# Two attention layers of a gated block: output projections as three reduced-precision products, Q two groups ahead in a ring

## What is computed

```python
x = x + tanh(g_xattn[0]) * attn0(layernorm(x), ctx)   # 16 heads of 32, biases
x = x + tanh(g_ffn[0])   * ffn0(layernorm(x))         # routed, 256 tokens a sequence
x = x + tanh(g_xattn[1]) * attn1(layernorm(x), ctx)   # 16 heads of 64
x = x + tanh(g_ffn[1])   * ffn1(layernorm(x))         # ternary weights, conv

def attn(x, ctx):                  # attn0 and attn1 alike
    q = x @ Wq;  k, v = ctx @ Wk, ctx @ Wv
    p = softmax(q @ k.T * dh ** -0.5)      # per head, over 128 context tokens
    return (p @ v) @ Wo + bo
```

## Time and profile before

| | us |
|---|---|
| median of 3 executions | 2031.3 |
| lowest, highest | 2029.82, 2041.83 |
| the profiled execution | 2034.14 |
| its span, first to last instruction | 2032.4 |
| PE busy in it | 1643.6 (81%) |
| DVE busy | 1249.5 (61%) |
| ACT busy | 817.9 (40%) |
| POOL busy | 542.0 (27%) |

### The profile page before, as it was taken

One profiled execution on the slowest core, in us unless ns is written; L12 is line 12 of the kernel. 1 busy time (PEld: TensorE's weight loads), 2 busy tenths in 40 slices (PEclk: granted clock), 3 DMA queues, 4 the chain that ended last, 5 costly groups with the idle time before them and its releaser, 6 DMA issues. The chain is left out here.

```text
span 2032.4 us, 23886 instructions
## 1 busy us (share of the span) xinstructions
PE 1643.6 (81%) x8804; PEld 876.0 (43%) x8804; DVE 1249.5 (61%) x1984; ACT 817.9 (40%) x1253; POOL 542.0 (27%) x472
## 2 busy tenths in 40 slices
PE   5788889884426788966999999999998557888887
PEld 3444444431203563425555555545443233444443
DVE  3577887785681343413546556556555449999996
ACT  3444444430561452304333233233222047777774
POOL 3122222220011210012121111111101048777771
PEclk9899998998667999987999999999999879999999
DMA  4012222112800243522011020110100140111121
GB/s 161 18 42 84 83 83 83 63 63 83 321 17 25 73 131 100 161 88 106 4 43 52 21 73 16 59 54 20 52 32 21 62 167 21 58 58 58 63 77 43
DMA packets 77666, 144.23 MB, mean 71 GB/s; under 512 B 12529, under 2 KB 21925, under 8 KB 77050
## 3 DMA queue, kind: packets, MB, share of 16 engines
q1 hardware_dynamic: 76602, 139.68, 20.0%
q0 software_dynamic: 960, 3.15, 0.5%
HBM read 99.78 MB, written 43.03 MB: 70 GB/s over the span
## 5 line engine op out<-in xcount | busy, mean ns | idle before, releaser
L561 PE MATMUL D_TX<-D_wo,D_oT 128*128 128x512 f32 x384 | 170.3, 597 | 2.5 <-DVE D_res L701 1.6
L515 ACT ACTIVATE D_probs<-D_SC 128x512 f32<-128x512 f32 x128 | 66.1, 603 | 223.1 <-PE D_SC L623 223.1
L1676 POOL TENSOR_TENSOR E_y<-E_y,E_centre 128x1024 f32<-128x1024 f32 x64 | 151.6, 2368 | 12.1 <-ACT E_y L1703 10.1
L1601 PE MATMUL E_OP<-E_w2q,E_yb 128*128 128x512 bf16 x512 | 130.5, 414 | 26.0 <-ACT E_yb L1688 21.8
L1592 PE MATMUL E_HP<-E_xT,E_w1q 128*128 128x512 bf16 x512 | 124.3, 387 | 9.0 <-DMA E_w1q<-w1b_d 6.1
L785 DVE TENSOR_TENSOR D_oT<-D_OB,D_rz 128x512 f32<-128x512 f32 x64 | 44.0, 688 | 133.3 <-PE D_OB L590 132.9
L1668 POOL TENSOR_SCALAR E_centre<-E_hs,E_cw,E_cb 128x512 f32<-128x512 f32 x64 | 107.8, 1684 | 63.9 <-DVE E_hs L1748 63.6
L552 PE MATMUL D_PJ<-D_xT_high,D_wq_high 128*128 128x512 f32 x236 | 101.9, 432 | 20.2 <-POOL D_xT_low L414 7.9
L419 POOL TENSOR_TENSOR D_rstd<-D_var,minus_half 128x1 f32<-128x1 f32 x32 | 17.4, 545 | 377.1 <-DVE D_var L707 377.1
L561 PEld LDWEIGHTS D_TX<-D_wo,D_oT 128*128 128x128 f32 x384 | 71.4, 191 | 85.3 <-issue 82.0
L1757 DVE SCALAR_TENSOR_TENSOR E_y<-E_hs,E_cw,E_y 128x512 f32<-128x512 f32 x128 | 107.2, 877 | 0.0
(11 more groups left out here) (332 smaller groups left out, 3739.8 us busy)
## 6 DMA issues: line engine op xcount, KB each, us to landing
A_x<-in_x SPq DMA_DIRECT2D x8, 1024.0 KB, 5.3
A_res<-in_x SPq DMA_DIRECT2D x8, 1024.0 KB, 5.8
x_d<-A_res SPq DMA_DIRECT2D x8, 1024.0 KB, 4.3
xn_d<-A_xn SPq DMA_DIRECT2D x8, 1024.0 KB, 8.3
W_raw<-in_w1T SPq DMA_DIRECT2D x16, 512.0 KB, 4.2
W_raw<-in_w2T SPq DMA_DIRECT2D x16, 512.0 KB, 4.2
D_x<-x_d SPq DMA_DIRECT2D x8, 1024.0 KB, 5.6
D_res<-x_d SPq DMA_DIRECT2D x8, 1024.0 KB, 5.7
```

What stands on the lines that cost most here:

```text
L515: act.activation(pr[:, g, :], SC[:, g, :], ACT.Exp, scale=scale).then_inc(s_ex, 1)
L561: mm = pe.matmul(out_banks[c], oT[par][:, k, c * P:(c + 1) * P], wo[:, k, :], start=k == 0, stop=k == QT - 1)
L1601: mm = pe.matmul(OP[:, :], yb[:, k, c * P:(c + 1) * P], w2q[:, k, :], start=k == 0, stop=k == MC - 1)
L1676: pool.tensor_tensor(y, y, U[i % 2][:, :, :], ALU.add).then_inc(t0, 1)
```

## The change

- **Output in three products.** Wo, scaled, is split into high (ACT) and low (POOL), the attention output too, and `project_out` makes three f32r matmuls where there was one in f32. The split of Wo is done in groups 0 and 1 of step 0.
- **Where the halves are made.** First layer: DVE divides into a buffer "o" of one tile, ACT makes the high half (`high_o`), POOL the low half (`low_o`). Second layer: DVE divides in place in bank OB, ACT makes the high half from it, DVE the low half; the next `weigh` may overwrite OB only then.
- **Second layer by halves of the heads.** A chunk of the output is now two units of four Q tiles' width each, added to the residual one after the other. Two units stand in each group, in banks ZB and PJ: at j == 2 and 3 the first half of this step, at j == 0 and 1 the second half of the step before. After step 7 four units are left.
- **Q two groups ahead.** Q is kept in a ring of 2 x QG tiles; group j makes Q of group j + 2. x of step n + 1 is transposed at j == 1 of step n, its statistics are taken at j == 3 and applied at j == 0, and x is loaded for step n + 2 after these transposes.
- **The lists.** ACT has high_o between guess_rz and keep_mT (in the second layer also one at the end of the group). POOL's list now goes by group. Ahead of step 0 only RING tiles of Q are made, and only the x of step 0 is transposed.

```diff
+        RING, OT = 2 * QG, QT // QG
+        woh, wol = sb("wo_high", [P, QT, D], F32R), sb("wo_low", [P, QT, D], F32R)
...
-        qh, ql = sb("q_high", [P, QT, TILE], F32R), sb("q_low", [P, QT, TILE], F32R)
-        oT = [sb(f"oT{i}", [P, QT, TILE]) for i in range(2)]
+        qh, ql = sb("q_high", [P, RING, TILE], F32R), sb("q_low", [P, RING, TILE], F32R)
+        oT = sb("oT", [P, 2, 2, OT, TILE], F32R)
+        of = sb("o", [P, TILE]) if QG == 1 else None
...
+        def q_ahead(lap, par, j):
+            return (2 * lap + par, lap, par, j + 2) if j < 2 else (2 * lap + par + 1, lap + par, par ^ 1, j - 2)
+        def out_units(lap, par, j):
+            if QG == 1:
+                return [(-1, 0, j, PJ[:, :] if j == 1 else TXF)]
+            back, half = (-1, 1) if j < 2 else (0, 0)
+            return [(back, half, 2 * (j % 2) + i, (ZB, PJ)[i][:, :]) for i in range(2)]
...
@@ sync, step @@
-                if not is_last(lap, par, 3):
-                    wait_apart(sp, x_tr, SUB * (n + 3), sp_passed)
-                    load_x(lap + 1 + par, par ^ 1)
+                if not is_last(lap, par, 2):
+                    wait_apart(sp, x_tr, SUB * (n + 2), sp_passed)
+                    load_x(lap + 1, par)
...
@@ gpsimd, step @@
+                for j in range(GROUPS):
+                    turn_x = j == 1 and not last
+                    if turn_x:
+                        low_x(n + 1, 0)
+                    if turn_x and QG == 1:
+                        low_x(n + 1, 1)
+                    if QG == 1:
+                        low_o(n, par, j)
+                    if turn_x and QG > 1:
+                        low_x(n + 1, 1)
+                    if first and j < 2:
+                        low_wo(j)
+                    if j == 0:
+                        add_bias(lap, par, (0, 1))
+                    if j == QG:
+                        add_bias(lap, par, (2, 3))
+                    if turn_x:
+                        low_x(n + 1, 2)
+                        low_x(n + 1, 3)
+                    if j == GROUPS - 1 and not is_last(lap, par, 2):
                         ln_rstd(n + 2)
                     if not first:
+                        for back, half, c, bank in out_units(lap, par, j):
+                            if half == QG - 1:
+                                post_rstd(n + back, c)
...
@@ scalar, step @@
+                    if more_q:
+                        keep_q(qn, QG * qj)
+                    if turn_x and QG == 1:
+                        keep_xT(n + 1, 0)
                     guess_rz(n, j)
+                    if isinstance(lap, int) and n == 0 and j < 2:
+                        split_wo(j)
+                    if QG > 1 and more_q:
+                        keep_q(qn, QG * qj + 1)
                     if turn_x:
+                        keep_xT(n + 1, 2 - QG)
+                    if turn_x and QG > 1:
+                        high_o(n, par, j, 0)
+                        keep_xT(n + 1, 1)
+                    if turn_x and QG == 1:
+                        high_o(n, par, j, 0)
+                        keep_xT(n + 1, 2)
+                    if not turn_x:
+                        high_o(n, par, j, 0)
                     if j < GROUPS - 1 or not last:
                         keep_mT(GROUPS * n + j + 1)
+                    if turn_x and QG > 1:
+                        keep_xT(n + 1, 2)
                     if turn_x:
+                        keep_xT(n + 1, 3)
+                    if QG > 1:
+                        high_o(n, par, j, 1)
...
@@ tensor @@
+            def project_out(i, k0, c, bank, part, parts):
+                for k in range(part * OT // parts, (part + 1) * OT // parts):
+                    for o, w in ((oh, woh), (oh, wol), (ol, woh)):
+                        mm = pe.matmul(bank, o[i][:, k, c * P:(c + 1) * P], w[:, k0 + k, :],
+                                       start=k == 0 and o is oh and w is woh, stop=k == OT - 1 and o is ol)
...
+                    if QG > 1:
+                        need(pe, fin, UNITS * n + 2 * j - SUB)
+                    if more_q:
+                        project_q(qn, QG * qj)
...
@@ vector, step @@
                     divide(n, par, j, 0)
+                    if j == 0 and not last:
+                        ln_apply(n + 1)
+                    if QG > 1:
+                        low_o(n, j, 0)
+                    if ahead and j == GROUPS - 1:
+                        ln_stats(n + 2, lap + 1, par)
+                    if QG > 1 and not first and j in (1, 2):
+                        for c in (2 * j - 2, 2 * j - 1):
+                            finish(*back1, c)
+                    for back, half, c, bank in [] if first and (QG == 1 or j < 2) else out_units(lap, par, j):
+                        add_out(n + back, par if back == 0 else par ^ 1, half, c, bank)
+                        if half == QG - 1:
+                            measure(n + back, par ^ 1, c)
+                    if QG == 1 and not first and j:
+                        finish(*back1, j - 1)
                     if QG > 1:
                         divide(n, par, j, 1)
+                        dve.wait_ge(o_ok, QT * n + QG * (j + 1))
+                        low_o(n, j, 1)
+                if not first and QG == 1:
+                    finish(*back1, SUB - 1)
```

More of the change, by code:

```diff
@@ L420, in post_rstd, with add_bias @@
                     .then_inc(p_rs, 1)
+            def add_bias(lap, par, chunks):
+                pool.wait_ge(r_in[par], 16 * (lap + 1))
+                for c in chunks:
+                    pool.tensor_tensor(R[par][:, c, :], R[par][:, c, :], bo[:, :], ALU.add).then_inc(biased, 1)
             ln_rstd(0)
@@ L432, in _, with low_wo @@
             pool.wait_ge(bo_ok, 1)
+            def low_wo(part):
+                for k in range(part * QT // 2, (part + 1) * QT // 2):
+                    pool.wait_ge(wo_hi, k + 1)
+                    pool.tensor_tensor(wol[:, k, :], wo[:, k, :], woh[:, k, :].bitcast(F32), ALU.subtract).then_inc(wo_lo, 1)
             def step(lap, par):
                 n = 2 * lap + par
-                first = isinstance(lap, int) and n == 0
-                for c in range(SUB):
-                    if c == 1 and not is_last(lap, par, 2):
+                first, last = isinstance(lap, int) and n == 0, is_last(lap, par, 1)
+                for j in range(GROUPS):
[18 more added lines that the diff above has]
+                    if j == GROUPS - 1 and not is_last(lap, par, 2):
@@ L670, in step @@
+                    if turn_x and not units:
+                        transpose_x(n + 1, 2)
+                        transpose_x(n + 1, 3)
+                    elif turn_x and QG == 1:
+                        transpose_x(n + 1, 3)
                     if QG > 1:
@@ L795, in _ @@
             maxima(0)
+            ln_stats(1, 0, 1)
             def step(lap, par):
```

246 lines of the change are left out of this document (132 added, 114 removed).

## The result

The changed kernel takes 2084.8 us in the median of four executions (2080.99 to 2087.73), beside 2032.9 for the kernel before: 1.0235 times as long, with a 95% interval of 1.0206 to 1.0263. The ratios of this document are those of means; the medians alone give 1.0255. The forecast was 2061, slower, range 2010 to 2095. The direction and the two mechanisms came true, the size of the loss in the first layer was too small.

The account below looks back on a forecast made before the run. PE bounds the second layer; in the first, PE and DVE are both near their limit. Second layer -24 and first +55 give +31, rounded to 30: 2064 us profiled, 2061 by the median, 1.5% slower; range 2010 to 2095.

Parts of the forecast that it names:

- the two mechanisms: First layer: POOL's wait for the residual closes a loop, and keep_mT waits on ACT behind high_o; layer sum +55 us.
- The loop of the first layer: Store, residual load, POOL's bias adds, low halves of x, Q, next store: binds steps 2 to 6 at 62.9 us each.
- the x loads: Sign of being right: in the first layer they come 62 to 64 us apart from step 2 on.
- Steps 0, 1 and 7 of the first layer: Step 0 goes from 45.2 to 59.1 us (+14), step 1 takes 53.1, step 7 and the end +3.
- The maxima behind the high half: First layer, ACT: keep_mT waits for divide and high_o, so a group takes 11.8 us instead of 10.56.
- The second layer: Sum -24 us: steps 1 to 6 -29, ahead of step 0 -17, step 0 +24, step 7 and the end -2.
- The products: Second layer: three f32r matmuls at 0.70 us replace one f32 at 0.886, -6.0 us a step.
- The wait for x: Second layer, j == 0: PE's wait for the last quarter of x goes away, -2.5 us a step.
- The new waits: Second layer: PE waits for late exps, 2.4 us after j == 1 and 1.3 after j == 2, +3.7 a step.
- The rival in which every group pays 1.4 us: First layer: idle PE lowers the clock in every group, 28 groups add 39 us, 2100 us in all; chance 0.15.
- Blocking of DVE by POOL: First layer: new low_o on POOL may hold DVE's last finish 1 us, 5 us more in all; left out of sum.
- The sentence on four passes: Output products: three of true FP32's four passes would make 0.66 us, 3 us more gain than 0.70; not used.

Follow-up runs that it names:

- the kernel with both edits of the first layer: Changed kernel; in the first layer POOL's bias adds end its step list and ACT copies transposed maxima ahead of o's high half: 2032.7 us, ratio 0.9975.

## Why the prediction was right, and where it was short

- *The loop of the first layer.* Right, term by term: store issued at +7.7 (forecast 7.7), residual in hand at +27.8 (27.1), last low half of x at +40.5 (39.0), low half of Q at +46.4 (44.2), next S at +53.1 (51.1), end of the step at +64.7 (62.9). Moving the bias adds takes it away and 46 us with it. Of the signs that it named, only the x loads missed, with 64 to 65 us between them instead of 62 to 64.
- *Its size.* The term that was too small is the sum after the residual is in hand: 11.9 us for POOL's list and 5.2 for the Q tile. POOL's items came to 12.6, because beside DVE's finish (1.38, 1.64, 1.76 us for its three parts) the low half of o took 1.73 us and the second pair of bias adds 2.93, instead of 1.27 and 2.5. The Q tile took 5.8 us, at the clock of 0.50 that the two holes had left. With 0.7 us more for the DMA that is 2.1 us, of which the last group gave 0.2 and the way from there to S 0.2 back; over steps 2 to 6 the excess is (65.2 - 62.9) x 5 = 12 us.
- *Steps 0, 1 and 7 of the first layer.* Step 0 was 64.6, forecast 59.1, its groups 14.0, 15.4, 20.7 and 14.5 against 13.8, 13.85, 19.65 and 11.8. Half of the excess is in the last group: PE without output products is often idle, has 2.8 us of idle time released by A_mT ahead of the next S and starts it at the slow clock (0.80 us for a first row that takes 0.51 at full clock). Step 1 was 56.5 (53.1); 2.3 us of that are its first group, whose S and first Q products ran at this clock. These 9 us are most of the rest of the miss. Their mechanism, the queue on ACT, is confirmed by the run that reorders ACT: step 0 falls by 9.6 us and step 1 by 2.6.
- *The maxima behind the high half.* Right: an ordinary group is 11.65 us from S to S (forecast 11.8, 10.56), with 1.34 us of idle PE released by A_mT. But within the loop the order costs only 0.9 us a step, as the same run shows.
- *The second layer.* -23 against a forecast of -24, by errors that cancel. The products gave 5.2 us of PE a step, not 6.0: a half chunk takes 2.89 us, so a chunk 5.78 against 7.09, and three f32r matmuls 0.72 with their starts, not 0.70. The run with one f32 product has PE busy 5.0 us longer and its step 4.0. The wait for x went (2.5). The new waits were 1.1 us a step and not 3.7: the finishes took 2.5 to 2.9 us, not 3.05, and at j == 2 nothing was late. A step won 5.8 us instead of 4.8. Step 0 cost 28 instead of 24, 9.0 us of it the wait for divide and low half behind the split of Wo, where I had 6.
- *The clock.* The rival in which every group pays 1.4 us did not happen: from 290 to 301 the clock is 1.00. It is low behind the two long holes of a step, and for a few us behind the 2.75 us at j == 0 (0.51 from 247.5 to 251), where the loop hides it.
- *Blocking of DVE by POOL.* I left it out of the sum. In the changed kernel that was nearly right, since DVE idles for 10.7 us behind it. It became the largest cost, 17 to 31 us, only once the loop was gone. The Trainium skill (SBUF — State Buffer, Who interferes with whom) gives as reason a pair of SBUF ports that DVE and GpSimd share, and excepts a DVE instruction with one SBUF input outside the two-port modes; the traces agree with both halves, 0.69 to 1.63 us for the product with two SBUF inputs, and no change for the statistics and for the low half of Q, which has one input in PSUM (0.75 us beside a POOL instruction too). The norm has one SBUF input and went from 0.54 to 1.48; that fits only if it ran in a two-port mode, which no trace here shows. The same section says that the second to issue is blocked until the first ends. Here both streams went on in turn, each instruction being held up for less than one of the other engine's: POOL's four adds took 6.24 us, against 4.96 for four without company (2.48 for two), which is 0.3 us more for each.
- *The sentence on four passes.* Its 3 us are a slip: 12 products in each of 32 chunks (8 in the second layer, 4 in the first) are 384, and at 0.70 less 0.66 us that is some 14 to 15. The 3 us were in no sum; measured, three f32r products take 0.72 us to the 0.886 of one in f32, 0.81 and not three quarters.

## What to carry to other kernels

When an instruction that waits for a DMA is moved in a queue, ask what stands behind it now, not what it costs itself: the same wait cost nothing at one place of POOL's list and 46 us at another. Follow such a wait around until it meets itself; if store, load and the work that ends in the next store form a loop, the step can't be shorter than the loop, and an engine inside it that is made faster (here ACT) gives back only what it takes from the loop, 0.9 us of 65 here. Compare each layer's new version with its old one as well as with the worst: here no version of the new first layer that does its whole work was shown to beat the old one. And once a loop is opened, look for what it had hidden before believing the sum: here two engines that hold each other up, where only what ran beside what mattered.

## What I had not expected of the hardware

- DVE and POOL slow each other at the same time. Two finishes and four bias adds, 3.7 and 5.0 us alone, took 7.6 and 6.2 us together. Statistics (2.46 us for four) and instructions with an input in PSUM (0.74) kept their time.
- A hole of 7.1 and one of 4.5 us on PE, 8 us apart, left it at a granted clock of 0.50, 1.2 GHz: ten matmuls of the following Q tile started 0.43 us apart instead of 0.233, so it cost 2 us behind the hole itself. Holes of 1.3 us in each group left the clock at 1.00. Behind a hole of 3.1 us it was 0.66 in one step of the kernel with both edits of the first layer, and 1.00 in one of the kernel that leaves the bias adds out.
- Half of the 14.1 us between a step's stores and the next load passed without a byte moved (251.5 to 258.5). Which of the three stores is the last to land, no run here shows.
